# The change of phase between attention and FFN: other places for x1's rows and pieces in SBUF, another order of the last attention step

## The reference

```
q, k, v = x @ Wq.T + bq, x @ Wk.T + bk, x @ Wv.T + bv      # q and k then turned by RoPE
qk  = einsum('bshd,bstd->bsht', q, k) / sqrt(32)           # heads against heads, at each position s
out = einsum('bsht,bstd->bshd', softmax(qk), v)            # then swapaxes(1, 2), reshape
x1  = layernorm(x + out @ Wo.T + bo)
g, u = (x1 @ gate_w.T) * gate_s, (x1 @ up_w.T) * up_s      # 512 -> 1408, weights -1, 0 or 1
y   = layernorm(x1 + ((silu(g) * u) @ down_w.T) * down_s)  # 1408 -> 512
```

## Time and profile before

| | |
|---|---|
| median of 3 runs (lowest to highest) | 1711.42 us (1709.96 to 1711.82) |
| profiled execution, its own time | 1709.7 us |
| its span, from the first to the last instruction | 1707.9 us |
| busy: PE, DVE, ACT, POOL | 97%, 77%, 58%, 38% of the span |
| mean granted TensorE clock | 0.989 |

### The profile page before, as it was taken

One profiled execution on the slowest core, in us unless ns is written; L12 is line 12 of the kernel. 1 busy time (PEld: TensorE's weight loads), 2 busy tenths in 40 slices (PEclk: granted clock), 3 DMA queues, 4 the chain that ended last, 5 costly groups with the idle time before them and its releaser, 6 DMA issues.

```text
span 1707.9 us, 40884 instructions
## 1 busy us (share of the span) xinstructions
PE 1658.1 (97%) x14946; PEld 1357.6 (79%) x14946; DVE 1321.2 (77%) x1936; ACT 983.1 (58%) x1585; POOL 641.5 (38%) x707
## 2 busy tenths in 40 slices
PE   6789999999999999998999999999999999999997
PEld 4578888888888888886788888888888888888886
DVE  6669999999999999997767676666676766767656
ACT  4556666666666666665545554555555545556454
POOL 7557666676666676662101101102011020110112
PEclk8989999999999999999999999999999999999999
DMA  6258878777777778788762544526535345354351
GB/s 204 65 139 197 183 171 188 182 168 185 174 184 189 170 179 182 174 182 212 232 202 85 184 155 139 166 92 196 174 107 180 111 153 168 97 193 144 100 182 65
DMA packets 438708, 275.53 MB, mean 161 GB/s; under 512 B 257280, under 2 KB 377216, under 8 KB 438656
## 3 DMA queue, kind: packets, MB, share of 16 engines
q1 hardware_dynamic: 438512, 274.61, 59.1%
q10 hardware_dynamic: 144, 0.26, 0.0%
HBM read 181.74 MB, written 93.06 MB: 161 GB/s over the span
## 4 chain that ended last, share of the span: by engine, by line
PE 93%; DVE 3%; issue 2%; POOL 1%; ACT 1%; DMA 0%; SPq 0%; POOLq 0%; DVEq 0%; ACTq 0%
PE ps_x L636 13%; PE ps_x L640 12%; PE ps_x L637 12%; PE ps_s L868 9%; PE ps_s L873 9%; PE ps_x L868 7%; PE ps_x L873 7%; PE ps_x L879 5%; PE ps_x L883 5%; PE ps_s L748 3%; PE ps_a L735 2%; PE ps_a L883 2%; PE ps_a L879 2%; PE ps_s L879 2%; PE ps_s L883 2%
## 5 line engine op out<-in xcount | busy, mean ns | idle before, releaser
L868 PE MATMUL ps_s<-x_hi,slot 128*128 128x512 f32 x672 | 264.2, 393 | 0.4
L873 PE MATMUL ps_s<-x_lo,slot 128*128 128x512 f32 x672 | 261.8, 390 | 0.0
L1495 POOL TENSOR_TENSOR z<-z,xr 128x512 f32<-128x512 f32 x60 | 77.3, 1314 | 480.7 <-DVE z L1850 480.7
L868 PE MATMUL ps_x<-x_hi,slot 128*128 128x512 f32 x560 | 219.1, 391 | 2.5 <-DVE x_lo L1836 1.1
L873 PE MATMUL ps_x<-x_lo,slot 128*128 128x512 f32 x560 | 218.0, 389 | 0.0
L1048 ACT ACTIVATE kX<-kT 32x512 f32<-32x512 f32 x256 | 161.3, 630 | 62.9 <-DVE kT L1601 49.4
L1781 DVE TENSOR_TENSOR hid<-ps_s,hid 128x512 f32<-128x512 f32 x88 | 60.8, 691 | 122.6 <-ACT hid L1192 122.6
L868 PEld LDWEIGHTS ps_s<-x_hi,slot 128*128 128x128 f32 x672 | 126.1, 188 | 34.7 <-ACT u L1223 4.2
L873 PEld LDWEIGHTS ps_s<-x_lo,slot 128*128 128x128 f32 x672 | 126.2, 188 | 25.3
L1340 POOL TENSOR_TENSOR s_lo<-x_sum,s_hi 128x256 fp32r<-128x256 f32 x128 | 94.7, 742 | 129.1 <-ACT s_hi L1040 129.1
L879 PE MATMUL ps_x<-wd,h 128*128 128x512 f32 x352 | 137.2, 390 | 0.2 <-DVE h L1822 0.2
(11 more groups left out here) (161 smaller groups left out, 4410.4 us busy)
## 6 DMA issues: line engine op xcount, KB each, us to landing
slot<-gu_hi SPq DMA_DIRECT2D x88, 896.0 KB, 5.1
xc<-x_cols SPq DMA_DIRECT2D x32, 512.0 KB, 3.8
v_rows<-v_in SPq DMA_DIRECT2D x32, 512.0 KB, 2.8
v<-v_rows SPq DMA_DIRECT2D x32, 512.0 KB, 5.2
res<-x_rows SPq DMA_DIRECT2D x64, 256.0 KB, 3.8
x_rows<-x_out SPq DMA_DIRECT2D x32, 512.0 KB, 3.8
x_cols<-x_turn SPq DMA_DIRECT2D x128, 128.0 KB, 2.5
raw<-x_cols SPq DMA_DIRECT2D x64, 256.0 KB, 5.2
```

Source lines behind the costliest of these rows:

```text
L868: pe.matmul(out[:, :], slot[:, WEIGHTS[i], cols], x_hi[:, i, k], start=start, stop=False, skip_group_check=True)
L873: last = pe.matmul(out[:, :], slot[:, WEIGHTS[i], cols], x_lo[:, i, k], start=False, stop=stop, skip_group_check=True)
L1495: pool.tensor_tensor(z[:, h, r], z[:, h, r], rows_of_x1(n, h)[:, r], ALU.add).then_inc(z_added[h], 1)
```

## The change

Six edits, all at the change of phase:

- **Places.** `wv_hi` goes ahead of `wb_hi`, so `raw`'s rows 4 to 7 lie over `wv_hi`, and `a_hi`, `a_lo`, `wv_lo` behind `wb_lo`. Within `wb_hi` and `wb_lo` the blocks stand in the order `B_AT`; `X_OVER` names the block under each piece (P1 over Q1, P2 over Q2, P6 over Q6, P5 over Q7, P7 over Q5, P4 over Q4, P3 over Q3), and `high_of_x` waits for that block only.
- **Loads.** Rows 0 to 3 go ahead of the load of v(30) and count in `raw_first`; rows 4 to 7 follow the store of x1(28) and wait for the last projection of v. t2 lies over `a_lo` and waits for Q4.
- **TensorE.** In step 31 Q5 comes ahead of `project_heads(29, 0)` and Q4 behind `weigh_values(30)`. Both halves of `project_heads(30)` come ahead of the scores of unit 31, in banks Y and W instead of W and Y.
- **ScalarE.** In step 31 P1 and P2 stand ahead of `spread_p(30)`; `top_of_slab(31)`, P7, the high part of heads(30) and P5 follow, then `spread_k(31, 1)`, P6 and `exponent(31)`.
- **VectorE.** The last step is written out: the q half ahead of the residual of unit 29, the low part of heads(30) ahead of the sums that need Q4 and Q3. Then the low parts of P1, P2 and P7 ahead of `subtract_top(31)`, P5 and P6 behind it.
- **Biases.** The semaphores of K's and V's bias become one.

Its core (the waits on `bias_...` and the index `B_AT[q]` in place of `q` at wb's other uses are left out):

```diff
+            wv_hi = sb("wv_hi", [P, KE, E], F32R, early)
+            wb_hi, wb_lo = (sb(name, [P, 7, KH, E], F32R, early) for name in ("wb_hi", "wb_lo"))
             a_hi, a_lo = (sb(name, [P, 2, KE, P], F32R, early) for name in ("a_hi", "a_lo"))
-            wb_hi, wb_lo = (sb(name, [P, 7, KH, E], F32R, early) for name in ("wb_hi", "wb_lo"))
-            wv_hi, wv_lo = (sb(name, [P, KE, E], F32R, early) for name in ("wv_hi", "wv_lo"))
+            wv_lo = sb("wv_lo", [P, KE, E], F32R, early)
...
+        B_AT = {Q1: 0, Q2: 1, Q6: 2, Q7: 3, Q5: 4, Q4: 5, Q3: 6}
-        bias_loaded = [sem(f"bias_loaded_{w}") for w in "qkv"]
+        bias_q_loaded, bias_kv_loaded = sem("bias_q_loaded"), sem("bias_kv_loaded")
-        X_FIRST = (P1, P2, P6, P5, P7, P4, P3)
+        X_FIRST = (P1, P2, P7, P5, P6, P4, P3)
+        X_OVER = (Q1, Q2, Q6, Q7, Q5, Q4, Q3)
...
                 if t == 4:
-                    sp.wait_ge(qk_done[Q4], UNITS)
+                    sp.wait_ge(v_done, 2 * UNITS)
                 sp.dma_start(raw[:, t // 4, t % 4], x1_cols[t].rearrange("f e q c -> (f e) (q c)"))\
-                  .then_inc(raw_loaded, 16)
+                  .then_inc(raw_first if t < ROWS else raw_loaded, 16)
...
                 load_slab(s)
+                if s == UNITS - 1:
+                    for t in range(ROWS):
+                        first_raw(t)
                 load_v(s - 1)
                 store_x1(s - 3)
                 if s == UNITS - 1:
-                    for t in range(4):
+                    for t in range(ROWS, T8):
                         first_raw(t)
                 store_v(s)
...
-            for t in range(4, T8):
-                first_raw(t)
             store_slab(UNITS - 1)
...
                 if ending:
-                    pe.wait_ge(y_done, 2 * (m - 1) + t + 1)
-                    pe.wait_ge(q0_made, UNITS)
+                    pe.wait_ge(y_done, 2 * (m - 1) + (2 if m == UNITS - 2 else t + 1))
+                    pe.wait_ge(q0_made, UNITS if t == 1 else UNITS - 1)
...
-                bank = (BANK_W, BANK_Y)[t] if ending else (BANK_Z, BANK_Y)[t]
+                bank = (BANK_Y, BANK_W)[t] if ending else (BANK_Z, BANK_Y)[t]
...
                 block_of_qk(Q7, u)
+                if last:
+                    block_of_qk(Q5, u)
                 project_heads(u - 2, 0)
-                block_of_qk(Q4, u)
-                block_of_qk(Q5, u)
+                if not last:
+                    block_of_qk(Q4, u)
+                    block_of_qk(Q5, u)
                 project_heads(u - 2, 1)
                 if last:
                     inputs_of_av(u - 1)
                     weigh_values(u - 1)
+                    block_of_qk(Q4, u)
                 block_of_qk(Q3, u)
...
             project_heads(UNITS - 2, 0)
-            inputs_of_score(UNITS - 1)
-            score(UNITS - 1)
             pe.wait_ge(lo_reduced, 1)
             pe.wait_ge(k1_made, UNITS)
             pe.matmul(ps_x[BANK_X][0:1, 0:1], lo_top1[:, :], ones[:, :], start=True, stop=True).then_inc(lo_joined, 1)
             project_heads(UNITS - 2, 1)
+            inputs_of_score(UNITS - 1)
+            score(UNITS - 1)
...
+            def high_of_x(n, i):
+                if isinstance(n, int) and n == 0:
+                    act.wait_ge(raw_first, 16 * ROWS)
+                    if i not in (P1, P2):
+                        act.wait_ge(raw_loaded, 16 * ROWS)
+                    act.wait_ge(qk_done[X_OVER[i]], UNITS)
+                else:
+                    act.wait_ge(raw_loaded, 16 * (T8 * n + ROWS))
+                if i in T_NEEDED:
+                    act.wait_ge(t_done, 4 * n + T_NEEDED[i])
+                at_least(act, p_done[i], NJ * n)
+                act.activation(even(x_hi[:, i]), OPERANDS[i], ACT.Copy).then_inc(bhi_done, 1)
...
                 high_of_slab(u)
-                if not ending:
+                if ending:
+                    high_of_x(0, P1)
+                    high_of_x(0, P2)
+                else:
                     high_of_sum(u + 1, Q7)
                 spread_p(u - 1)
-                if not ending:
+                if ending:
+                    top_of_slab(u)
+                    high_of_x(0, P7)
+                    high_of_heads(u - 1)
+                    high_of_x(0, P5)
+                else:
                     high_of_tile(u + 1, 1)
                     high_of_sum(u + 1, Q5)
                 spread_k(u, 1)
...
                 if first:
-                    high_of_heads(UNITS - 2)
-                    top_of_slab(UNITS - 1)
-                    high_of_x(0, P1)
-                    high_of_x(0, P2)
+                    high_of_x(0, P6)
                     exponent(UNITS - 1)
-                    high_of_x(0, P6)
-                    high_of_x(0, P5)
-                    high_of_x(0, P7)
                     act.wait_ge(late_loaded, 16 * 3)
...
             def first_sums_of_x():
-                pool.wait_ge(raw_loaded, 16 * T8)
+                pool.wait_ge(raw_first, 16 * ROWS)
+                pool.wait_ge(raw_loaded, 16 * ROWS)
                 pool.wait_ge(v_done, 2 * UNITS)
...
                 pool.wait_ge(t_done, 2)
+                pool.wait_ge(qk_done[Q4], UNITS)
                 pool.tensor_tensor(even(t2), B22, T1, ALU.subtract).then_inc(t_done, 1)
...
                 turn_prob(u - 1)
+                if isinstance(u, int) and u == UNITS - 1:
+                    q_of_second(u)
+                    turn_q(u, 1)
+                    turn_x1(u - 3)
+                    add_residual(u - 2, (0,))
+                    add_residual(u - 2, (1,))
+                    low_of_heads(u - 1)
+                    k_of_second(u)
+                    turn_k(u, 1)
+                    q_of_first(u)
+                    turn_q(u, 0)
+                    return
                 turn_x1(u - 3)
...
-            with dve.Fori(OPENING, UNITS) as i:
+            with dve.Fori(OPENING, UNITS - 1) as i:
                 step(i)
-            begin_step(UNITS)
+            step(UNITS - 1)
...
                 if first:
-                    low_of_heads(UNITS - 2)
                     aggregate(UNITS - 3)
                     dve.wait_ge(lo_seen, SLABS)
                     dve.tensor_reduce(lo_top1[:, :], lo_top[:, :], AX.X, ALU.max).then_inc(lo_reduced, 1)
-                    subtract_top(UNITS - 1)
+                    low_of_x(0, P1)
                     dve.wait_ge(lo_joined, 1)
                     dve.tensor_scalar(all_exact[0:1, :], ps_x[0][0:1, 0:1], 0.0, None, ALU.is_equal).then_inc(flag_set, 1)
-                    low_of_x(0, P1)
                     low_of_x(0, P2)
+                    low_of_x(0, P7)
+                    subtract_top(UNITS - 1)
+                    low_of_x(0, P5)
                     low_of_x(0, P6)
-                    low_of_x(0, P5)
                     sum_t(0, 3)
-                    low_of_x(0, P7)
```

More of the change, by code:

```diff
@@ L242, in post_ln_layer @@
         dscale_loaded, pw_set = sem("dscale_loaded"), sem("pw_set")
-        raw_loaded = sem("raw_loaded")
+        raw_loaded, raw_first = sem("raw_loaded"), sem("raw_first")
         slot_loaded = [sem(f"slot_loaded{i}") for i in range(3)]
@@ L365, in load_bias @@
                 sp.dma_start(bias[:, b], biases[b:b + 1, :].to_broadcast([P, E]))\
-                  .then_inc(bias_loaded[b] if b < 3 else late_loaded, 16)
+                  .then_inc({WQ: bias_q_loaded, WO: late_loaded}.get(b, bias_kv_loaded), 16)
             def x_view(buffer):
@@ L673, in block_of_qk @@
                 for k in range(KH):
-                    last = three(ps_x[QK_BANK[q]][:, :], hi[:, k], lo[:, k], wb_hi[:, q, k], wb_lo[:, q, k],
+                    last = three(ps_x[QK_BANK[q]][:, :], hi[:, k], lo[:, k], wb_hi[:, B_AT[q], k], wb_lo[:, B_AT[q], k],
                                  k == 0 and q in (Q1, Q2, Q5), k == KH - 1, ahead if k == KH - 1 else None)
@@ L1018, in high_of_block @@
                     act.wait_ge(B_MADE[q], 1)
-                act.activation(wb_hi[:, q], B_RAW[q], ACT.Copy).then_inc(b_hi_done, 1)
+                act.activation(wb_hi[:, B_AT[q]], B_RAW[q], ACT.Copy).then_inc(b_hi_done, 1)
             def high_of_tile(m, t):
@@ L1233, in high_of_hid2 @@
                 act.activation(h_hi[slot_h2(j)][:, :], hid2[:, j], ACT.Copy).then_inc(h2hi_done, 1)
-            def high_of_x(n, i):
-                act.wait_ge(raw_loaded, 16 * T8 * (n + 1))
-                if isinstance(n, int) and n == 0:
-                    act.wait_ge(qk_done[Q3], UNITS)
-                if i in T_NEEDED:
-                    act.wait_ge(t_done, 4 * n + T_NEEDED[i])
-                at_least(act, p_done[i], NJ * n)
-                act.activation(even(x_hi[:, i]), OPERANDS[i], ACT.Copy).then_inc(bhi_done, 1)
             def normalise(n, h):
@@ L1525, in low_of_block @@
                 dve.wait_ge(b_hi_done, B_ORDER.index(q) + 1)
-                dve.tensor_tensor(wb_lo[:, q], B_RAW[q], wb_hi[:, q].bitcast(F32), ALU.subtract)\
```

(21 more changed lines are left out.)

2 lines of the change are left out of this document (1 added, 1 removed).

## The result

Slower: the median went from 1709.73 to 1714.28 us (19 runs of each), a ratio of 1.0024 (95% interval 1.0015 to 1.0033); by the ratio that is about 4.1 us. The forecast was 1710.5, made from a median of before of 1711.42 (three runs), and the measured time lies 1.3 us above its range. The profiled execution of after took 1712.2 us, with a span of 1710.4 (before 1709.7 and 1707.9).

A forecast was written before the change was run, and what follows sets the result against it. Steady attention keeps TensorE busy, so only the change of phase, with 6.6 us of loss, could give. A 2.3 us gain less 1.4 for the clock left 0.9: 1708.8 in the trace, plus 1.7 makes 1710.5 us; range 1707.8 to 1713.0.

The forecast's parts named there:

- Loads: SyncE at the phase change: rows 0 to 3 land by about 779.8, rows 4 to 7 issue from 777.2, landing at 785.4.
- L: Landing time of x1 rows 4 to 7, called the quantity that decides: taken as 785.4, between 783.6 and 787.9.
- the upper L of 787.9: Latest landing estimated for rows 4 to 7, from 3 MB taking 14.4 us at the earlier rate.
- spread_p's cover: ScalarE before values(30): spread_p(30), behind P1 and P2, ends at 784.4, leaving 0.8 us to spare.
- Heads of 30: First projection of heads(30): starts at 791.0 after a 1.3 us wait, takes 2.75 us without a clock fall.
- The flag and scores(31): TensorE after heads(30,0): flag matmul waits 0.4 us, second projection goes first, scores(31) run 797.1 to 798.8, 0.2 us later.
- Products: FFN products after scores(31): P6 at 803.7 after a 3.0 us wait, P4 at 808.5, gain 2.3 us if clock stays.
- The hole of 3 us: TensorE idle in front of P6, waiting for its low part on VectorE behind subtract_top(31): 3.0 us.
- The clock again: Clock falls after the 3.0 us wait at P6, costing 1.4 us and leaving a gain of 0.9 us.
- Costed at nothing: Several effects given no time, among them VectorE low parts beside GpSimd's three sums, with 1.5 us of cover.
- the gain of 0.9 us: Net forecast gain at the phase change: 2.3 us less 1.4 us for the clock's fall.
- Chances: Odds on the whole result: faster by about 0.2% 0.18, slower beyond that 0.10, within 0.72.

The follow-up runs named there:

- rows ahead: Kernel after, with SyncE's loads of rows 4 to 7 put ahead of the store of x1(28): ratio 1.0005 to the kernel before.
- lows first: Kernel after, with VectorE's low parts of P5 and P6 ahead of subtract_top(31) and ScalarE's copy of s1 ahead of exponent(31): ratio 1.0015.
- slots late: Kernel after, with only SyncE's loads of slots 1 and 2 held until scores(31) are done: ratio 1.0009.
- the 40 added matmuls: Kernel after, with 40 matmuls of one column and one row added on TensorE ahead of heads(30,0): ratio 1.0015.
- heads first with slots late: Kernel after, with ScalarE's high part of heads(30) ahead of P7 and the loads of slots 1 and 2 held until scores(31) are done: ratio 1.0003.
- the faster version: Kernel after: high part of heads(30) before P7, low parts of P5 and P6 before subtract_top, slots 1 and 2 and unit 30's residual rows held behind scores(31): 0.9984.
- slots late in the kernel before: Control: kernel before, with the loads of slots 1 and 2 held until scores(31) are done: ratio 0.9998.

## Why the prediction was wrong

Two terms of the sum failed: scores(31) were given no stop in their new place, and the hole ahead of heads(30,0) was taken too short to bring the lower clock.

- *Loads, right by two errors that cancelled.* Rows 4 to 7 were to go out at 777.2 and went at 779.65, since the store of x1(28) ahead of them kept SyncE for 4.18 us. They landed in 6.2 us, not 8.2: t3 at 785.83 against L = 785.4. So L came out by luck. They landed behind v(30) (781.7) and x1(28) (783.1), in the order of issue, but the upper L of 787.9 was not reached. Values(30) were not held; spread_p's cover stood (it ended at 782.9).
- *Heads of 30: mis-sized.* Heads(30,0) were forecast for 791.0 and came at 791.40, by the chain forecast. But TensorE was free 0.65 us sooner than I took, since this execution came to the stage that much sooner, and the rows did not. So the hole was 2.36 us, not 1.3, and the step "so 2.75 us are due for the projection" failed: it took 4.51 us, 1.75 us lost to the lower clock. A hole of 1.3 us was not met; behind 0.84 and 1.01 us (rows ahead, lows first) the clock did not fall.
- *The flag and scores(31): the step that failed.* The text has them "start at 797.1 and end at 798.8", 1.7 us, as they took before. That duration belonged to the old place, where a piece of code was fetched 0.3 us before they began and the next boundary lay in the slow matmuls of heads(30,1) behind them (272 instructions behind heads(30,0)). In the new place the boundary lies six matmuls from their end. They ended at 802.9, 3.9 us from start to end. The flag's wait of 0.4 us did not come.
- *Products: right.* From the end of scores(31) to P6 4.9 us, as forecast. The hole of 3 us was not seen at P6, because P1 came 0.70 us behind the scores and P1 and P2 ran at half clock (0.50), 0.43 us a matmul; with the stop away (slots late) P6 waits 2.05 us for x_lo there.
- *The clock again: right in size, not in place.* The clock fell, but at 802.6, behind the stop, before P6 was reached; from P6 to P4 5.69 us against 4.8, 0.9 in place of 1.4. Behind a wait of 2.05 us at P6 it did not fall in slots late (1.00 from 810 to 815 us), and fell with the 40 added matmuls (0.50 from 809 to 811 us). So it is luck that one fall was due.
- *Costed at nothing.* VectorE's work beside GpSimd's three sums kept its length: the transpose of kT took 1.09 us beside them, and 1.05 before, when GpSimd stood.
- *The sum.* Counted from the end of the stop in scores(30), P4 came 3.3 us later than before (44.5 us against 41.2), where 1.0 less was forecast (809.9 against 810.89): a miss of 4.3 us. Of this 1.1 lie ahead of heads(30,0), since the rows came that much later against TensorE. From heads(30,0) to P4 I forecast 17.5 us and 1.4 for the fall; measured were 22.06, 3.2 more: 1.75 for the clock in the projection, 1.89 for the stop, less 0.5. By the medians the miss is about 5 us (a ratio of 0.9995 forecast, 1.0024 measured); what one execution of each doesn't show of that stays open. No run shows the gain of 0.9 us itself: heads first with slots late, where the clock's fall and most of the stop are out, takes 0.9 us less than before from scores(30) to values(31), but in another order on ScalarE; slots late alone, in the order of the change, takes 35.6 us from heads(30,0) to values(31) against 34.9 before, with the low clock in heads(30,0) in both (0.63 from 795.4 to 800 us, 0.73 from 791 to 796 us before).
- *Chances.* Slower had 0.10, and what the trace "can't show" was sought on VectorE. The trace did show the kind: the kernel before has such a stop in scores(30), as every kernel here has (1.4 to 2.4 us), in rows that the prediction made no use of, while in the loop such scores run through:

```profile
742.92 1.62 PE L748 MATMUL ps_s<-kX,qT 64*32 64x64 f32 x126
...
766.67 1.40 PE L748 MATMUL ps_s<-kX,qT 64*32 64x64 f32 x107
769.68 0.46 PE L748 MATMUL ps_s<-kX,qT 64*32 64x64 f32 x19 [1.61 <-issue]
```

The difference is in the code: from 110 to 680 us, where TensorE goes round the loop, no packet comes on this queue in the kernels before and after (one at most in the others), and step 31 is written out behind the loop. From 130 to 755 us TensorE has not one hole named issue.

What stays open: what sets off a fetch, and so how long a stop is. The stop's place is shown to be one of the code. Three pairs (4.85 to 1.11, 1.89 to 0, 2.39 to 0) speak for a length that follows the loads in flight, but each length is from one profile, and the ranges overlap: with this order on TensorE the stop was 1.89 to 4.85 us with slots 1 and 2 in flight, and 0 to 2.39 us with them held. Full engines don't always hold a fetch: in the kernel before and with the 40 added matmuls the packet started among transfers that filled them (share 1.07 and 1.29 in the half us ahead of it). In the faster version some of the gain may be from other waits than the stop.

## What to carry to other kernels

When many small matmuls are moved, their duration need not move with them: ask whether their code is run for the first time, how many instructions stand between them and the last slow work, and which DMAs are in flight, for code comes by DMA too (here in packets of 16 KB). A stop named after no releaser in the trace of before is worth a term in the sum when work of the same kind is moved. And when a wait is removed without gain, look for what took the gain back: with the hole ahead of heads(30,0) gone, the stop grew from 1.89 to 4.85 us, and with the stop gone, P6 stood for a low part queued behind subtract_top.

## What the runs showed of the hardware

- TensorE's code arrives by DMA in packets of 16 KB (28 packets and 0.46 MB on that queue in every run), and TensorE outran it: 122 small matmuls in 1.59 us, then 1.1 to 4.9 us of standstill. It did so in code that it came to for the first time; round the loop no packet came from 110 to 680 us in the kernels before and after, at most one in the others, and it did not stop (the scores at 742.92 in 1.62 us). The place moved by 24 matmuls when 48 instructions were added, and stayed 272 instructions behind heads(30,0) when the order was changed. Two stops in one run, 3.21 and 1.37 us, stand 256 instructions apart (slots late in the kernel before).
- The packet itself takes 0.9 to 1.4 us, and TensorE resumes 2.3 to 2.9 us after its start (the stops in scores(31) and heads(30,1)). Among the slot loads of 896 KB it started at 799.8 in the kernel after, 0.8 us behind the start of scores(31). With these held in the changed kernel it started as the engines fell idle in four runs (share 0.93 to 1.00, then 0.16 to 0.64 in the last half us ahead of it); in the fifth, slots late alone, it started 1.7 us after that.
- The store of x1(28), issued in 1.24 us at 775.34 before, took SyncE 4.18 us right behind rows 0 to 3 and the load of v(30), and held rows 4 to 7 behind it.
